# Attention scores as three rounded row-tiled products, column-tiled state products and a third input buffer in a linear-attention + mixture-of-experts kernel

## What is computed

```python
q = elu_feature_map(proj(Wq)); k = elu_feature_map(proj(Wk)); v = proj(Wv)   # elu(x) + 1
def step(carry, qkv):                       # one row after the other
    kv_sum = kv_sum + jnp.einsum('bhd,bhe->bhde', k_i, v_i)
    k_sum = k_sum + k_i
    num = jnp.einsum('bhd,bhde->bhe', q_i, kv_sum)
    den = jnp.sum(q_i * k_sum, axis=-1, keepdims=True)
    out_i = num / (den + EPS)
x = x + out @ Wo.T
x = x + moe(layernorm(x))
```

## Time and profile before

| | |
|---|---|
| median of 3 runs | 1032.64 us (1032.32 to 1032.79) |
| the profiled execution | 1031.95 us, of it 1030.2 us from the first to the last instruction |
| PE busy | 1007.4 us (98% of the span) |
| DVE busy | 838.3 us (81%) |
| POOL busy | 537.6 us (52%) |
| ACT busy | 422.3 us (41%) |

### The profile page before, as it was taken

One profiled execution on the slowest core, in us unless ns is written; L12 is line 12 of the kernel. 1 busy time (PEld: TensorE's weight loads), 2 busy tenths in 40 slices (PEclk: granted clock), 3 DMA queues, 4 the chain that ended last, 5 costly groups with the idle time before them and its releaser, 6 DMA issues.

```text
span 1030.2 us, 22106 instructions
## 1 busy us (share of the span) xinstructions
PE 1007.4 (98%) x8437; PEld 859.6 (83%) x8437; DVE 838.3 (81%) x1776; ACT 422.3 (41%) x750; POOL 537.6 (52%) x440
## 2 busy tenths in 40 slices
PE   6889999999999999999999999999999999999997
PEld 5768888888888888888888888888888888888886
DVE  4888888888978889898788978889888888977554
ACT  5754343434434344343434434344343434422222
POOL 5864545556354463545556345463545556343643
PEclk9999999999999999999999999999999999999999
DMA  5011425345252543425345253444424345231321
GB/s 204 3 47 57 104 63 137 66 117 110 62 144 60 137 83 105 109 58 139 67 114 111 59 142 70 135 83 104 107 64 136 66 121 114 59 107 58 102 82 42
DMA packets 235160, 96.48 MB, mean 94 GB/s; under 512 B 161712, under 2 KB 217520, under 8 KB 235056
## 3 DMA queue, kind: packets, MB, share of 16 engines
q1 hardware_dynamic: 235056, 95.07, 36.1%
HBM read 66.60 MB, written 28.44 MB: 92 GB/s over the span
## 4 chain that ended last, share of the span: by engine, by line
PE 90%; DVE 3%; ACT 2%; DMA 2%; issue 1%; POOL 1%; SPq 0%; DVEq 0%; ACTq 0%; POOLq 0%
PE bank L997 55%; PE y_bank L997 19%; PE bank L1106 6%; PE bank L1122 5%; PE bank L1093 2%; PE bank L1136 2%; PE bank L1148 1%; DMA cw_all<-in_w_qkvo 1%; DMA x_dram<-blocks 0%; DMA cw_all<-cw_dram 0%; DMA expo<-x_dram 0%; ACT wg_hi L580 0%; DVE et L965 0%; DVE x_mid L990 0%; ACT expo L641 0%
## 5 line engine op out<-in xcount | busy, mean ns | idle before, releaser
L997 PE MATMUL bank<-xt_hi,wg_hi 128*128 128x512 f32 x576 | 237.4, 412 | 3.0 <-DVE et L965 2.3
L746 POOL TENSOR_TENSOR h_lo<-et,h_hi 128x512 fp32r<-128x512 f32 x142 | 180.9, 1290 | 96.6 <-ACT h_hi L696 96.4
L997 PE MATMUL bank<-xt_lo,wg_hi 128*128 128x512 f32 x576 | 228.5, 397 | 0.0
L997 PE MATMUL bank<-xt_hi,wg_lo 128*128 128x512 f32 x576 | 228.5, 397 | 0.0
L743 POOL TENSOR_TENSOR et<-et,cw_all 128x512 f32<-128x512 f32 x124 | 163.5, 1339 | 115.1 <-DVE et L971 97.6
L871 DVE TENSOR_TENSOR scores<-bank,cst 128x512 f32<-128x512 f32 x240 | 152.6, 681 | 41.4 <-PE bank L1106 34.1
L997 PE MATMUL y_bank<-wd_hi,h_hi 128*128 128x256 f32 x576 | 165.0, 286 | 0.3 <-POOL h_lo L746 0.3
L997 PE MATMUL y_bank<-wd_hi,h_lo 128*128 128x256 f32 x576 | 161.5, 280 | 0.0
L997 PE MATMUL y_bank<-wd_lo,h_hi 128*128 128x256 f32 x576 | 161.4, 280 | 0.0
L997 PEld LDWEIGHTS bank<-xt_hi,wg_hi 128*128 128x128 f32 x576 | 108.6, 189 | 40.5 <-issue 16.8
L965 DVE SCALAR_TENSOR_TENSOR et<-et,bank 128x512 f32<-128x512 f32 x144 | 95.9, 677 | 48.7 <-ACT et L687 48.6
(11 more groups left out here) (131 smaller groups left out, 1830.5 us busy)
## 6 DMA issues: line engine op xcount, KB each, us to landing
cw_all<-cw_dram SPq DMA_DIRECT2D x124, 256.0 KB, 3.9
x_dram<-blocks SPq DMA_DIRECT2D x112, 128.0 KB, 3.3
out_y<-x_mid SPq DMA_DIRECT2D x32, 256.0 KB, 4.6
x_in<-in_x SPq DMA_DIRECT2D x15, 512.0 KB, 4.8
num_t<-x_dram SPq DMA_DIRECT2D x15, 512.0 KB, 4.1
expo<-x_dram SPq DMA_DIRECT2D x13, 512.0 KB, 4.0
k_dram<-blocks SPq DMA_DIRECT2D x52, 96.0 KB, 2.6
k_tok<-k_dram SPq DMA_DIRECT2D x13, 384.0 KB, 3.4
```

The costliest lines, as they stand in the source:

```text
L746: nc.gpsimd.tensor_tensor(h_lo[:, i % HR, :], et[:, i % ET, :], h_hi[:, i % HR, :].bitcast(f32), ALU.subtract).then_inc(h_lo_done, 1)
L997: ins = nc.tensor.matmul(dst, l, r, start=first and n == 0, stop=last and n == 2, skip_group_check=shared)
```

## The change

From batch 2 on, `scores` no longer multiplies float32 operands. ACT's new `k_split` rounds `kf` to `k_hi`, POOL's new `k_split` makes `k_lo`; ACT's `q_split` writes the rounded `q_hi`, and DVE's new `q_split` makes the two halves of `q_lo` by two instructions. PE then makes three products (hi*hi, hi*lo, lo*hi), still in row tiles. The state products and `inter` go to the four column tiles of 32: 12 products of 128 by 32 in place of three of 128 by 128 in `state`, four for each one in `inter`. `x_in` has three buffers in place of two. Batches 0 and 1 keep the float32 scores, with `q_half` now lying in `blocks`. Some waits of the start are made finer. The lists of PE and SP are unchanged, those of ACT, POOL and DVE have 28 new entries each and are otherwise in the same order.

```diff
-ET, HR, CW, SM, XB = 3, 3, 4, 8, 2
+ET, HR, CW, SM, XB = 3, 3, 4, 8, 3
...
     "ACT": """
...
-        k.1.0 q.0.0 at.0.1 q.1.0 q_split.0.0 split.0.2 v.1.0 split.2.2 v.0.0 split.1.2 gate.4.2 gate.3.2
+        k.1.0 k_split.0.0 q.0.0 at.0.1 q.1.0 k_split.1.0 q_split.0.0 split.0.2 v.1.0 split.2.2 v.0.0 split.1.2 gate.4.2 gate.3.2
...
     "POOL": """
...
-        take.2.2 take.3.2 weigh.8.3 weigh.7.3 split.8.3 split.6.3 split.7.3 take.1.0 take.0.0 qk.0.0 qk.1.0
+        take.2.2 take.3.2 weigh.8.3 weigh.7.3 split.8.3 split.6.3 split.7.3 take.1.0 take.0.0 qk.0.0 k_split.0.0 qk.1.0 k_split.1.0
...
+        k_hi, k_lo = (sb(f"k_{n}", [P, KC, S], f32r) for n in ("hi", "lo"))
+        q_hi, q_lo = (sb(f"q_{n}", [P, 2, S], f32r) for n in ("hi", "lo"))
...
+                elif name == "k_split":
+                    act.wait_ge(drained[BANK["k", i]], USES["k", i, b])
+                    wait_filled(act, "scores", 8 * i + 3, b - 1)
+                    wait_filled(act, "scores", 8 * i + 7, b - 1)
+                    nc.scalar.activation(k_hi[:, i, :], kf[:, i, :], ACT.Copy).then_inc(k_hi_done, 1)
...
+                elif name == "k_split":
+                    pool.wait_ge(k_hi_done, K_HI["k_split", i, b])
+                    nc.gpsimd.tensor_tensor(k_lo[:, i, :], kf[:, i, :], k_hi[:, i, :].bitcast(f32), ALU.subtract)\
+                        .then_inc(k_lo_done, 1)
...
+                elif name == "q_split":
+                    dve.wait_ge(q_half_done, Q_HALF["q_split", i, b])
+                    for j in range(2):
+                        last = nc.vector.scalar_tensor_tensor(q_lo[:, j, :], qf[:, i, :], cst[:, C_EO + j:C_EO + j + 1],
+                                                              q_hi[:, j, :].bitcast(f32), ALU.mult, ALU.subtract)
+                    last.then_inc(q_lo_done, 1)
...
                     for c in range(SUBS - 1):
...
                         for g in range(4):
                             rows = slice(32 * g, 32 * g + 32)
                             last = nc.tensor.matmul(
+                                bk[rows, c * 2 * DH:(c + 1) * 2 * DH].rearrange("p (t d) -> p t d", d=DH),
+                                k_tok[:, i, c, rows], v_win[:, c, i * 4 + g, 0:3:2, :],
+                                start=True, stop=True, skip_group_check=True)
...
+                        pe.wait_ge(k_lo_done, K_LO["k_split", m, b])
+                        pe.wait_ge(q_lo_done, Q_LO["q_split", m, b])
+                        pairs = ((k_hi, q_hi[:, :, :]), (k_hi, q_lo[:, :, :]), (k_lo, q_hi[:, :, :]))
...
-                        last = nc.tensor.matmul(bank[BANK["o", m]][:, c * P:(c + 1) * P], st[:, m, c - 1, :],
-                                                qf[:, m, c * P:(c + 1) * P], start=False, stop=True,
-                                                skip_group_check=True)
+                        for g in range(4):
+                            rows = slice(32 * g, 32 * g + 32)
+                            last = nc.tensor.matmul(bank[BANK["o", m]][rows, c * P:(c + 1) * P], st[:, m, c - 1, rows],
+                                                    qf[:, m, c * P:(c + 1) * P], start=False, stop=True,
+                                                    skip_group_check=True)
```

More of the change, by code:

```diff
@@ L82 @@
         ln1_apply.0.2 gate.1.0 wide.0.1 mask.15.1 gate.2.0 turn.0.2 gate.0.0 piece.9.0 wide.1.1 route.0.0
-        at.0.1 turn.1.2 k.0.2 q.0.2 split.0.0 q_split.0.2 k.1.2 at.1.1 v.1.2 k_turn.0.2 v.0.2 q.1.2 split.1.0
+        at.0.1 turn.1.2 k.0.2 q.0.2 split.0.0 q_split.0.2 k_split.0.2 k.1.2 at.1.1 v.1.2 k_turn.0.2 v.0.2 q.1.2 k_split.1.2 split.1.0
         gate.3.0 gate.4.0 split.2.0 k_turn.1.2 wide.0.2 gate.5.0 q_split.1.2
@@ L364, in linear_attention_moe @@
         q_half_done, Q_HALF = sem("q_half_done"), nth("ACT", ("q_split",), 2)
+        k_hi_done, K_HI = sem("k_hi_done"), nth("ACT", ("k_split",))
+        k_lo_done, K_LO = sem("k_lo_done"), nth("POOL", ("k_split",))
+        q_lo_done, Q_LO = sem("q_lo_done"), nth("DVE", ("q_split",))
+        UNSPLIT = min(b for _, _, b in K_HI)
         rden_wide, WIDE = sem("rden_wide"), nth("ACT", ("wide",))
@@ L425, in wait_blocks @@
                 wait_for(eng, put_done, 64 * n)
+            else:
+                for j in range(4):
+                    wait_filled(eng, "scores", j, UNSPLIT - 1)
         def wait_weighed(eng, i, b):
@@ L537, in _ @@
                     if b == 0:
-                        wait_split(sp, NP - 1)
+                        for n in range(NS, NP):
+                            wait_split(sp, n)
                     if b == B - 1 and i >= CW:
@@ L849, in _ @@
                     wait_filled(dve, "inter", 2 * i + 1, b - 1)
[L850 to L853, removed]
+                    nc.vector.tensor_tensor(st[:, i, :, :].rearrange("p c (g n) -> p c g n", g=4),
+                                            bank[BANK["state", i]][:, 0:(SUBS - 1) * 2 * DH]
+                                            .rearrange("p (c n) -> p c n", n=2 * DH).unsqueeze(2)
+                                            .broadcast_to([P, SUBS - 1, 4, 2 * DH]),
+                                            block_mask.rearrange("p (g n) -> p g n", g=4).unsqueeze(1)
+                                            .broadcast_to([P, SUBS - 1, 4, 2 * DH]), ALU.mult)\
                         .then_inc(drained[BANK["state", i]], 1)
@@ L1099, in _ @@
                     m, c0 = i // 2, 2 * (i % 2)
-                    pe.wait_ge(drained[BANK["k", m]], USES["k", m, b])
-                    pe.wait_ge(q_half_done, Q_HALF["q_split", m, b])
+                    if ("k_split", m, b) in K_LO:
+                        pe.wait_ge(k_lo_done, K_LO["k_split", m, b])
+                        pe.wait_ge(q_lo_done, Q_LO["q_split", m, b])
+                        pairs = ((k_hi, q_hi[:, :, :]), (k_hi, q_lo[:, :, :]), (k_lo, q_hi[:, :, :]))
+                    else:
+                        pe.wait_ge(drained[BANK["k", m]], USES["k", m, b])
+                        pe.wait_ge(q_half_done, Q_HALF["q_split", m, b])
+                        pairs = ((kf, q_half),)
                     for j in range(2):
                         cs = slice((c0 + j) * P, (c0 + j + 1) * P)
[L1104 to L1111, removed]
+                        for n, (keys, queries) in enumerate(pairs):
+                            for g in range(4):
+                                rows = slice(32 * g, 32 * g + 32)
+                                last = nc.tensor.matmul(
+                                    bank[BANK["scores", 4 * i + g]][:, j * 2 * P:(j + 1) * 2 * P]
+                                    .rearrange("p (h q) -> p h q", h=2),
+                                    keys[rows, m, cs], queries[rows, :, cs],
+                                    start=n == 0, stop=n == len(pairs) - 1)
+                                if j == 1 and n == len(pairs) - 1:
+                                    last.then_inc(filled, 1)
                 elif name == "values":
```

33 lines of the change are left out of this document (17 added, 16 removed).

## The result

The changed kernel takes **1126.72 us** (median of four runs, 1125.8 to 1127.63), the kernel before 1032.48 us on the same chip (1032.22 to 1032.79): ratio 1.0913 (95% interval 1.0894 to 1.0932). The forecast was 1052 us, its range ended at 1066: the sign was right, the size was not. The profiled execution took 1126.98 us.

A forecast was written before the change was run, and what follows sets the result against it. PE was taken as the bound, busy 1007.4 of 1030.2 us. Per turn, steps -0.75, `q.1` +0.45 and `scores.0` +1.8 make +1.5, times 13 turns +19.5, giving 1052 us; range 1043 to 1066.

The forecast's parts named there:

- What PE's steps occupy: PE's changed steps: scores -0.16 us each, state -0.12 each, `inter.2` with `inter.3` +0.32, `inter` with `scores.3` -0.03.
- the second rival: State step bound by records, not data: 0.44 us more for each of 32 steps, +14, 1066 us; chance 0.13.
- the third: Rival: rounded products in row tiles run at float32 pace, 0.6 more for each of 56 steps, 1085 us; chance 0.05.
- `q.1`: PE's start of `q.1`, delayed through ACT's rounding of `k.0` and DVE's `qf`: +0.45 us a turn, including the `inter` loss.
- ACT's time at `scores.0`: With the second rounding of keys, ACT's split of the queries ends 3.05 us after `q.1`.
- DVE's two subtractions: Ahead of `scores.0`, two of 0.69 us, 1.29 together; `scores.0` starts 4.5 us after `q.1`, PE stands 1.8 us.
- DVE is free: Ahead of `scores.0`, DVE was taken as free for the two subtractions, having begun `result` at 461.06.
- What else is added is covered: POOL's two extra subtractions a turn and DVE's `q_lo` of half 1 (1.3 us) priced as covered; 0.3 us if not.
- The clock: PE's window over twelve turns was at full granted clock; the sum had no term for a lower clock.
- The start: The third x buffer and the finer waits of the start were taken as worth 0.

The follow-up runs named there:

- the tail: The changed kernel plus repeated `q_lo` instructions after its last work: 0.75 us alone, 1.75 beside POOL subtractions, 0.74 beside POOL with one operand in PSUM.
- filling it: The changed kernel with PE's `up.4` ahead of `scores.0`, and `v.0` ahead of `v.1`: 1089.05 us, ratio 1.0586.
- five copies: The kernel before with five ACT copies of `qf` that nobody reads, ahead of the queries' split: 1078.78 us, ratio 1.0464.
- two copies: The kernel before with two ACT copies of `qf` that nobody reads, ahead of the queries' split: 1044.46 us, ratio 1.0131.

## Why the prediction was wrong, by its steps

- **What PE's steps occupy: right.** Scores -0.16 each (measured -0.163), rounded products in row tiles 0.12 us a group, `inter.2` with `inter.3` +0.33 (+0.32). State -0.17 where -0.12 was taken. So the second rival (a state step bound by records) and the third (the float32 pace) fell.
- **`q.1`: right.** +0.51 for +0.45 (0.46 by means), and moving ACT's entry gives 0.44 of it back.
- **ACT's time at `scores.0`: right to 0.01 us** (3.04 us after `q.1`), but ACT was not the latest there: DVE reached `q_lo` 0.5 us behind it.
- **DVE's two subtractions, the step that failed.** The prediction priced them at 0.69 us each, the median of the earlier trace rows, and took that DVE is free. The same group has the maximum, 1.84, and the prediction quoted it, yet used it only for 0.05 of a microsecond and a bound. Both prices stood in the trace of before, and putting the group's rows beside POOL's timeline would have told them apart (below). Beside POOL `q_lo` costs 1.75 us (the tail). DVE's `cum` ahead of it, which reads two operands from SBUF as well, took 2.07 us beside `k_lo`; 13 of the 32 of the run took 2.06 to 2.08, and the mean is 1.60 where it was 1.26 before. The pair ended 0.5 + 1.0 us later than taken, so the wait is 3.2, above the bound of 2.5. POOL waiting for `q_lo` gave 1.0 of it back.

  "DVE is free" had little room even before: there DVE ran `cum`, the transposes and `qf` without a gap to 461.14, 2.71 us after `q.1`, only 0.34 us ahead of the 3.05 at which ACT was to be ready. The 0.85 us that `cum` lost is more than that.

```profile
458.42 1.22 DVE L864 TENSOR_TENSOR_SCAN cum<-cst,kf 128x512 f32<-128x512 f32 x1
459.55 1.01 DVE L844 STREAM_TRANSPOSE blocks<-kf 128x384 f32<-128x384 f32 x2
460.49 0.65 DVE L827 SCALAR_TENSOR_TENSOR qf<-bank,expo 128x512 f32<-128x512 f32 x1
```

  The kernel before, two of the 28 subtractions of the earlier trace rows on DVE's timeline:

```profile
154.34 1.75 DVE L901 TENSOR_TENSOR at_lo<-num_t,at_hi 128x512 fp32r<-128x512 f32 x1
...
472.09 0.69 DVE L901 TENSOR_TENSOR at_lo<-num_t,at_hi 128x512 fp32r<-128x512 f32 x1
```

  and POOL's timeline around them:

```profile
154.25 3.00 POOL L743 TENSOR_TENSOR et<-et,cw_all 128x512 f32<-128x512 f32 x2
...
468.02 2.53 POOL L746 TENSOR_TENSOR h_lo<-et,h_hi 128x512 fp32r<-128x512 f32 x2 [1.25 <-ACT h_hi L696]
474.72 3.80 POOL L743 TENSOR_TENSOR et<-et,cw_all 128x512 f32<-128x512 f32 x3 [4.16 <-DVE et L971]
```

  The slow one lies inside POOL's work, the fast one in POOL's gap from 470.55 to 474.72. Of the 28, the 15 with POOL idle all took 0.68 to 0.69 us; of the 13 beside POOL five took 1.5 to 1.84 and eight 0.68 to 0.82. So POOL beside it can make it slow and does not always.
- **"What else is added is covered": wrong twice.** POOL's two subtractions a turn were hidden from PE by POOL's idle time, but not from DVE, which they slow. And `q_lo` of half 1 was taken as 1.3 us behind 1.17 us of slack; it took 3.4 and gave 2.0 us a turn at `scores.2` and `scores.3`, as moving it showed.
- **The clock: left out.** The sum priced PE's work behind the stand at full clock because the trace of before had no low clock in the turns. A stand of this length has a second bill, 1.5 us a turn here. The copies showed that a stand alone can do it, and filling it showed the bill going away.
- **The start: taken as 0, was 8.3 us.** The wait for `k_lo` at the first rounded scores is seen, 3.8 us; the rest, other waits for DVE and POOL and a stretch of half clock, was not taken apart by a run.

By terms the miss is, in a turn, 1.5 us at `scores.0`, 2.0 at `scores.2` and `scores.3`, 1.5 of clock: 5.0 × 13 = 65, with 8 us of start 73 of the 75 us between 1052 and 1127.

## What to carry to other kernels

Price a DVE instruction by its neighbour as well as by its form: if both its operands are in SBUF and POOL will work on SBUF at the same time, take the upper duration of the group as the bound, for that instruction and for those already there; idle time on POOL is no cover for DVE. Where a change makes PE stand still for microseconds, add the price of the low clock behind the stand, and look first for work in PE's own list that can go ahead of the wait: that one move was worth more here than any change on the engine that was late. Try the parts of a change alone: of three, one (`state` in column tiles) gained 0.4%, one (`inter`) cost what the first had gained, and the rounded scores cost all the rest.

## What the runs showed of the hardware, not expected

- A DVE subtraction of 128x512 goes from 0.75 to 1.75 us beside POOL, and POOL's from 1.25 to 1.7; with one of DVE's operands in PSUM neither is slowed.
- Behind a stand of PE of 2.2 to 3.2 us the granted clock was 0.50 for 3.4 us, in all 13 at 3.2 in the changed kernel but in 9 of 13 at the same 3.2 with `q_lo` of half 1 early, in 9 of 13 at 2.5 (five copies), in 7 of 13 at 2.2 (POOL waits), and in none at 0.9 (two copies) and 0.8 (`up.4` first). In some turns it lasted 6.8 us.
- 24 products of 32 columns in four column tiles end within 0.33 us, 14 ns each. The Trainium skill (TensorE: Matmul & The Clock Gate, Wait — 56ns, not 53.3ns?) says that starts are never less than about 25 ns apart; for products in different column tiles this row contradicts it (four of them start within 0.02 us).
- Rounded products in four row tiles take 0.12 us for a group of 256 columns, the time of one such product on the whole array.
